# A step of an attention stage laid out anew: key, output and router projections in other slots, and the router's search with them

## The chip, the cores and the metric

The kernel runs on one core of a Trainium2 chip. The metric is the device time of one execution in microseconds (us), lower is better. Engines: TensorE (PE, matmul), VectorE (DVE), ScalarE (ACT), GpSimd (POOL), SyncE (SP, which here only issues DMAs).

## The reference, cut to what matters

One decoder layer over 16 batches of 256 tokens, width 256, three post-norm blocks in fp32:

```python
u = einsum('bld,nd->bln', x, B); h = scan(h = A*h + u)             # state
x = layernorm(x + h @ W.T + b)                                     # first norm: x1
q, k, v = proj(x, Wq, bq), proj(ctx, Wk, bk), proj(ctx, Wv, bv)    # 16 heads of 16
q, k = rotary(q), rotary(k)
scores = where(|i - j| <= 50, q @ k.T / 4, -1e9)
x = layernorm(x + softmax(scores) @ v @ Wo.T + bo)                 # second norm: x2
probs = softmax(silu(x @ router_w1) @ router_w2, over the tokens)
weights, tokens = top_k(probs, 64)                                 # for each of 16 experts
x = layernorm(x + scatter(weights * expert(x[tokens])))            # 16 gated MLPs
```

## The kernel before, in words

The kernel has two stages. `mixing` computes everything up to x2 and the router for the first eight batches; `experts` then runs 2 x 16 units of expert matmuls. The change lies in `mixing` alone.

`mixing` is a software pipeline written by hand. Its iteration is a **step** `i` (from -2 to 16), and each step has 16 **slots** `t`, one for a head. Every engine runs `step(it)` in a program of its own, strictly in order; semaphores join them. A name in `DELAY` says which batch an operation works on: U and Y (the state's input projection and its output projection) are two batches ahead of the heads, X (transpose of x1), K, Q, V one ahead, O (output projection), OX (transpose of x2) and R (router's first matmul) two behind. So K, Q, V exist in steps -1 to 14, U and Y in steps -2 to 13, and O, OX, R from step 2 on. Steps 2 to 9 are two passes of a hardware loop over four steps; the others are written out.

In slot `t` PE does, in this order: the scores of head t (`heads`, line 589, two matmuls into `score[t % 2]`, once DVE has finished head t-2); in slots 1, 5, 9, 13 the transpose of a group's maxima (`turn_maxima`, line 602); the transposed scores of head t-9 (`turned_heads`, lines 616 and 618); in slots 2, 6, 10, 14 a `gather` of probabilities times values (line 636); and then the slot's projection, if it has one.

All projections share two PSUM banks, `work[0]` and `work[1]`. `ORDER` (line 258) gives the cyclic order of the users of each bank, and `begin(it, name)` makes PE wait for `freed` of the user ahead of it in that order. These are freed by: K and Q by ACT's two bias activations (`biased`, line 841, `raw_k`, `raw_q`), X and OX by ACT's copies (line 856), O and Y by DVE's first addition in `statistics` (line 953), U by DVE's scan (line 1014), V by DVE's two additions into `vp` (line 1039), R by ACT's copy into `r1` (line 905).

The slots before: X 0, K 1, Q 3, O half in 4 and half in 7, U 5, Y 8, V 11, OX 13, R 15. The second norm's chain is: DVE `statistics` 8, ACT `estimate` 9 (log and exponential), POOL `inverse_deviation` (five operations on 128x2 elements), DVE `normalise` 11 (writes `x2cur`), PE OX 13, ACT x2T 14, PE R 15, ACT r1 15. `NORMAL` (line 318) holds these numbers, `DRAIN` those of the last step.

ACT's order in a slot: `keep_maxima` (slots 1, 5, 9, 13: copies the maxima that PE turned and issues a DMA with them), the exponential of head t-9 (line 787), and then the copies and bias activations of the slot: x1T in slot 1, K's bias in 2, Q's in 4, K's high half in 5, Q's in 7.

DVE's order: the maxima of head t (line 945, two pairs), in slots 3 and 11 the sums of the odd group (lines 994 to 1000), then the rotation of K (slot 3, lines 977 and 982) and of Q (5), the scan (6), the norms' statistics (O 8, Y 9) and normalisations (O 11, Y 13), and V (12).

POOL's order in a step: x1 plus a bias, x plus a bias, `cosine` and `rotate` of K, `cosine` and `rotate` of Q, `lower` of K, `lower` of Q (the low halves, line 468), the inverse sums of the even pair, the deviations of O and Y, the inverse sums of the odd pair. SP loads the next inputs, copies the halves of K and Q into their stacks (line 390) and stores x2 (line 423).

The router's search runs once inside this pipeline: ACT's silu over eight batches (step 10, slot 9), sixteen PE passes for the logits (step 11, slot 13, line 712), DVE's maximum (11, 14), ACT's exponential (12, 1), and eight rounds of `take_eight` on DVE (lines 121 to 124) from step 12 to 15.

Of the kernel before, what the change touches and what calls it, by code (L numbers as in the profile page):

```python
# [28 lines left out]
P = 128  # L29
NB = 16  # L30
S = 256
# [146 lines left out]
def mixing(nc, dram, keep):  # L178
# [5 lines left out]
    with ExitStack() as ctx:  # L184
# [73 lines left out]
        ORDER = (("X", "Q", "U", "Y", "OX"), ("K", "O", "V", "R"))  # L258
# [59 lines left out]
        NORMAL = {"O": (4, 7), "statistics": 8, "estimate": 9, "normalise": 11, "OX": 13, "x2T": 14, "R": 15, "r1": 15}  # L318
        DRAIN = {"O": (1, 2), "statistics": 2, "estimate": 3, "normalise": 5, "OX": 6, "x2T": 7, "R": 8, "r1": 9}

        def slot(it):
            return DRAIN if it.fixed and it.i >= NB else NORMAL

# [121 lines left out]
        def _(pool):  # L445
# [54 lines left out]
            def step(it):  # L500
                behind = it.batch(-1)
                if it.batch(0):
                    bias_residual(it)
                if there(it, "U"):

                    par = it.r % 2
                    pool.wait_ge(x_in[par], it.pairs(32, 2))
                    if not it.at_least(-1):
                        pool.wait_ge(const_in["b_mix"], 16)
                    else:  # L510
                        pool.wait_ge(x1_ready, it.lin(1, 2))
                    nc.gpsimd.tensor_tensor(xb[:], xin[par][:], b_mix[:].unsqueeze(1).to_broadcast([P, TT, D]),
                                            ALU.add).then_inc(xb_ready, 1)
                if it.fixed and it.i == -2:
                    pool.wait_ge(const_in["rope"], 32)
                    cosine(FIRST_KEYS, 0)
                    rotate(FIRST_KEYS, 0)
                if there(it, "K"):
                    if not hoisted(it):
                        cosine(it, 0)  # L520
                        rotate(it, 0)
                    cosine(it, 1)
                if there(it, "Q"):
                    rotate(it, 1)
                    if not hoisted(it):
                        lower(it, 0)
                    lower(it, 1)
                drain = it.fixed and it.i >= NB
                if drain and there(it, "O"):
                    inverse_deviation(it, "O")  # L530
                if behind:
                    inverse_sums(it, -2)
                if there(it, "O") and not drain:
                    inverse_deviation(it, "O")
                if there(it, "Y"):
# [30 lines left out]
        def _(pe):  # L566
# [99 lines left out]
            def step(it):  # L666
                for t in range(NH):
# [6 lines left out]
                    if t == 1 and there(it, "K") and not hoisted(it):  # L674
                        keys(it)
                    if t == 6 and it.fixed and it.i == -2:
                        keys(FIRST_KEYS)
                    if t == 0 and there(it, "X"):
                        first_use(it, "X", "ident")
                        pe.wait_ge(x1_ready, it.lin(1, 2))  # L680
                        transposed(it, "X", x1[(it.r + 1) % 4])
                    if t == 3 and there(it, "Q"):
                        first_use(it, "Q", "wq")
                        pe.wait_ge(freed["X"], uses(it, "X"))
                        project(it, "Q", wq, x1T)
                    if t in slot(it)["O"] and there(it, "O"):
                        n = slot(it)["O"].index(t)
                        if n == 0:
                            begin(it, "O")
                            pe.wait_ge(attnT_ready, it.lin(NPAIR, -NPAIR))  # L690
                        for g in range(NPAIR):
                            mm = nc.tensor.matmul(bank("O")[:, n * D:(n + 1) * D], attnT[it.r % 2][:, g, n * P:(n + 1) * P],
                                                  wo[:, g, :], start=(g == 0), stop=(g == NPAIR - 1))
                        if n == TT - 1:
                            mm.then_inc(ready["O"], 1)
# [11 lines left out]
                    if only(it, 11, t, 13):  # L707
                        pe.wait_ge(rw2_set, 1)
                        pe.wait_ge(silu_done, 1)
                        pe.wait_ge(freed["V"], uses(it, "V"))  # L710
                        for c in range(GB):
                            mm = nc.tensor.matmul(bank("R")[:, 0:S], rw2_placed[:, c, :], r1[:, c * S:(c + 1) * S],
                                                  start=(c == 0), stop=(c == GB - 1))
                        mm.then_inc(logits_ready, 1)
                    if only(it, NB - 1, t, 10):
# [16 lines left out]
                    if t == slot(it)["R"] and there(it, "R"):  # L732
                        if it.fixed and it.i == 11:
                            pe.wait_ge(logits_kept, 1)
# [7 lines left out]
                        mm.then_inc(ready["R"], 1)  # L742

# [16 lines left out]
        def _(act):  # L760
# [97 lines left out]
            def step(it):  # L858
                for t in range(NH):
# [3 lines left out]
                    if t == 2 and there(it, "K") and not hoisted(it):  # L863
                        biased(it, 0)
                    if it.fixed and it.i == -2 and t == 7:
                        biased(FIRST_KEYS, 0)
                    if t == 1 and there(it, "X"):
                        columns(it, "X", x1T)
                    if t in (7, 15):
                        keep_values(it, t)  # L870
# [6 lines left out]
                    if t == 5 and there(it, "K") and not hoisted(it):  # L877
                        heighten(it, 0)
# [6 lines left out]
                    if only(it, 10, t, 9):  # L885
# [4 lines left out]
                    if only(it, 12, t, 1):  # L890
# [25 lines left out]
        def _(dve):  # L916
# [68 lines left out]
            def step(it):  # L985
                for t in range(NH):
                    maxima(it, t)
                    if t in (3, 11) and has(it, group(t, 15)) and not only(it, NB, t, 11):

                        p = group(t, 15) // 2  # L990
# [10 lines left out]
                    if t == 3 and there(it, "K") and not hoisted(it):  # L1001
                        rotated(it, 0)
# [42 lines left out]
                    if only(it, 11, t, 14):  # L1045
# [4 lines left out]
                    if only(it, 12, t, 2):  # L1050
                        scale_probabilities(dve, route)
                    for n, (i, at) in enumerate(((12, 7), (12, 14), (13, 1), (13, 14), (14, 1), (14, 14), (15, 1), (15, 4))):
# [790 lines left out]
```

## Time and profile before

| | |
|---|---|
| median of 3 runs | 1072.51 us (1072.12 to 1072.58) |
| profiled execution: its own time, and its span | 1072.09 us, 1070.3 us |
| PE busy | 991.9 us (93%) |
| PE weight loads | 845.4 us (79%) |
| DVE busy | 729.6 us (68%) |
| POOL busy | 672.7 us (63%) |
| ACT busy | 591.3 us (55%) |
| mean granted PE clock | 0.975 |

The span is that of the profiled execution from its first to its last instruction; the own time is the device time of the same execution. Busy shares are means over both stages.

### The profile page before, as it was taken

What the parts mean: (1) busy time and instruction counts of PE and PEld (TensorE: products, weight loads), DVE (VectorE), ACT (ScalarE), POOL (GpSimd) and SP (SyncE); (2) the same over time, 40 slices, a digit from 0 to 9 for tenths busy, and PEclk for the clock granted to TensorE, in tenths of its full rate; (3) what the DMA queues carried; (4) which work ended last, traced back from release to release, by engine and by line L of the source; (5) the groups of instructions that cost most, each with busy time, mean ns of one, the idle gap of its engine ahead of it and who ended that gap; (6) DMA issues with size and microseconds to landing.
All of it is one profiled execution on the core that took longest, in us unless ns stands there. A gap on an engine that the chain in (4) does not pass through costs nothing.

```text
span 1070.3 us, 21269 instructions
## 1 busy us (share of the span) xinstructions
PE 991.9 (93%) x6436; PEld 845.4 (79%) x6436; DVE 729.6 (68%) x2168; ACT 591.3 (55%) x1234; POOL 672.7 (63%) x784
## 2 busy tenths in 40 slices
PE   4799999999989998879999999999999999999990
PEld 3578778777877877658898888888888888888880
DVE  4678888888877798757554787565556756765633
ACT  1155565556565555456656555555555556555642
POOL 5556666666666565267757665776666767666543
PEclk8899999999999999899999999999999999999995
DMA  6344344433333332525676666666676666666636
GB/s 191 84 103 98 100 106 103 103 99 102 102 101 97 85 81 70 182 94 168 156 223 124 160 141 168 136 158 152 160 218 158 141 155 149 147 155 143 184 54 176
DMA packets 114918, 142.56 MB, mean 133 GB/s; under 512 B 15104, under 2 KB 88064, under 8 KB 114688
## 3 DMA queue, kind: packets, MB, share of 16 engines
q1 hardware_dynamic: 86432, 105.56, 34.2%
q0 software_dynamic: 24576, 33.57, 18.1%
q10 hardware_dynamic: 3808, 2.22, 0.7%
q8 instruction: 45, 0.74, 0.3%
q14 instruction: 57, 0.47, 0.1%
HBM read 90.70 MB, written 29.36 MB: 112 GB/s over the span
## 4 chain that ended last, share of the span: by engine, by line
PE 52%; ACT 1%; DMA 1%; POOL 1%; issue 1%; DVE 0%; ACTq 0%; POOLq 0%; SPq 0%
PE gate_bank L1349 16%; PE attn L1349 16%; PE value_bank L1349 16%; PE turn_bank L1359 2%; DMA last<-acc_rows 0%; ACT last L1590 0%; DMA acc_rows<-y,slots_now 0%; PE attn L1432 0%; PE attn L1406 0%; POOL acc_rows L1294 0%; DVE stats L1627 0%; DVE hidden L1620 0%; ACTq L1594 0%; ACT w_hi L1482 0%; POOL rstd L167 0%
## 5 line engine op out<-in xcount | busy, mean ns | idle before, releaser
L1294 POOL DMA_INDIRECT acc_rows<-y,slots_now x128 | 205.6, 1607 | 137.4 <-issue 73.4
L787 ACT ACTIVATE probsT<-scoreT 128x356 f32<-128x356 f32 x256 | 117.7, 468 | 137.6 <-PE scoreT L618 113.3
L945 DVE CUSTOM_DVE_ANT_0 scored<-score,band 128x178 f32<-128x178 f32 x512 | 149.9, 337 | 63.3 <-PE score L589 59.4
L1620 DVE TENSOR_TENSOR hidden<-gate,value_bank 128x512 f32<-128x512 f32 x128 | 87.9, 687 | 152.7 <-ACT gate L1495 152.6
L1495 ACT ACTIVATE gate<-gate_bank 128x512 f32<-128x512 f32 x128 | 76.6, 598 | 188.3 <-PE value_bank L1349 188.3
L1349 PE MATMUL attn<-w_hi,h_hi 128*128 128x256 f32 x512 | 146.1, 285 | 0.2
L1349 PE MATMUL attn<-w_hi,h_lo 128*128 128x256 f32 x512 | 143.3, 280 | 0.0
L1349 PE MATMUL attn<-w_lo,h_hi 128*128 128x256 f32 x512 | 143.3, 280 | 0.0
L589 PE MATMUL score<-k_stack,q_stack 96*128 96x178 f32 x512 | 123.8, 325 | 7.2 <-DVE nmax L945 4.2
L589 PEld LDWEIGHTS score<-k_stack,q_stack 96*128 96x128 f32 x512 | 88.9, 194 | 37.1 <-DVE nmax L945 17.3
L618 PE MATMUL scoreT<-q_stack,k_stack 97*128 97x356 f32 x256 | 116.5, 456 | 0.0
L1612 DVE TENSOR_TENSOR h_lo<-hidden,h_hi 128x512 fp32r<-128x512 f32 x128 | 88.2, 689 | 21.5 <-ACT h_hi L1499 21.1
L1349 PEld LDWEIGHTS attn<-w_lo,h_hi 128*128 128x128 f32 x512 | 97.2, 190 | 3.2
L1349 PE MATMUL gate_bank<-k_stack,q_stack 128*128 128x512 f32 x384 | 99.1, 393 | 0.5 <-PEq L184 0.5
L1349 PEld LDWEIGHTS attn<-w_hi,h_hi 128*128 128x128 f32 x512 | 96.3, 188 | 3.8 <-ACT y L1509 0.3
L1349 PE MATMUL value_bank<-k_stack,q_stack 128*128 128x512 f32 x384 | 97.4, 389 | 0.0
L1349 PEld LDWEIGHTS attn<-w_hi,h_lo 128*128 128x128 f32 x512 | 96.2, 188 | 0.0
L1276 POOL DMA_INDIRECT rows<-x_rows,rows_now x64 | 76.7, 1199 | 28.0 <-issue 14.3
L1602 DVE TENSOR_TENSOR w_lo<-arena,w_hi 128x1024 fp32r<-128x1024 f32 x64 | 79.8, 1247 | 21.1 <-ACT w_hi L1482 20.9
L1499 ACT CAST h_hi<-hidden 128x512 fp32r<-128x512 f32 x128 | 78.9, 617 | 23.3 <-DVE hidden L1620 23.3
L616 PE MATMUL scoreT<-band_bf,ident_bf 128*128 128x356 bf16 x256 | 83.8, 327 | 5.9 <-ACT probsT L787 3.2
L1276 POOL DMA_INDIRECT arena<-x_rows,rows_now x60 | 71.6, 1193 | 26.9 <-issue 14.0
(214 smaller groups left out, 2374.9 us busy)
## 6 DMA issues: line engine op xcount, KB each, us to landing
arena<-in_w SPq DMA_DIRECT2D x96, 512.0 KB, 4.0
k_stack<-high_k SPq DMA_DIRECT2D x128, 64.0 KB, 2.2
q_stack<-high_q SPq DMA_DIRECT2D x128, 64.0 KB, 2.3
arena<-in_xT SPq DMA_DIRECT2D x16, 256.0 KB, 2.9
arena<-in_x SPq DMA_DIRECT2D x16, 256.0 KB, 3.1
arena<-in_cT SPq DMA_DIRECT2D x16, 256.0 KB, 3.7
k_stack<-low_k SPq DMA_DIRECT2D x64, 64.0 KB, 2.3
q_stack<-low_q SPq DMA_DIRECT2D x64, 64.0 KB, 2.2
```

The lines of the kernel that those rows point to most:

```text
L589: mm = nc.tensor.matmul(score[t % 2][:, q * SPAN:(q + 1) * SPAN], q_stack[par][0:TOP, t // 2, t % 2, q * P:(q + 1) * P], k_stack[par][0:TO ...
L616: nc.tensor.matmul(out, ident_bf[:], band_bf[:, k, :].unsqueeze(1).to_broadcast([P, 2, SPAN]), start=True, stop=False)
L618: nc.tensor.matmul(out, k_stack[par][0:TOP + 1, f, k * P:(k + 1) * P], q_stack[par][0:TOP + 1, f, :, k * FIRST:k * FIRST + SPAN], start=Fa ...
L787: nc.scalar.activation(probsT[g % 2][:, u % HG, :, :].rearrange("p a s -> p (a s)"), scoreT[u % 2][:, 0:2 * SPAN], ACT.Exp, scale=1.0 / DH ...
L945: op = nc.vector.tensor_tensor_reduce(scored[t % 2][:, q, :], score[t % 2][:, q * SPAN:(q + 1) * SPAN], band[:, q, :], -1.0, BIG, ALU.add, ...
L1276: nc.gpsimd.indirect_dma_start(rows[it.par][:, m, :], None, dram["x2"][it.h], bass.IndirectOffsetOnAxis(ap=now[:, m:m + 1], axis=0)).then_ ...
L1294: nc.gpsimd.indirect_dma_start(dram["acc"][c], bass.IndirectOffsetOnAxis(ap=now[:, m:m + 1], axis=0), y[m][:], None, compute_op=ALU.add).t ...
L1349: mm = nc.tensor.matmul(out, a[x], b[z], start=(n == 1), stop=(n == 3 * len(pairs)))
L1499: nc.scalar.copy(h_hi[it.par][:, f, :], hidden[f % 2][:]).then_inc(h_hi_ready, 1)
L1602: nc.vector.tensor_tensor(w_lo[it.par][n][:], raw[n], w_hi[it.par][n][:], ALU.subtract).then_inc(w_lo_ready[n], 1)
L1612: nc.vector.tensor_tensor(h_lo[it.par][:, f, :], hidden[f % 2][:], h_hi[it.par][:, f, :], ALU.subtract).then_inc(h_lo_ready, 1)
L1620: nc.vector.tensor_tensor(hidden[f % 2][:], gate[f % 2][:], value_bank[f % 2][:], ALU.mult).then_inc(hidden_ready, 1)
```

## The change: what it does

- K moves from PE's slot 1 to slot 0, behind X; ACT's bias of K from slot 2 to 1 (behind x1T), its high half from 5 to 3, DVE's rotation of K from slot 3 to 2.
- O moves whole into slot 2, with statistics in 3, estimate in 4, normalise in 7, OX in 9, x2T in 10, R in 13 and r1 in 14.
- OX moves from the first bank's order to the second's, behind O: K, O, OX, V, R.
- The odd group's sums move from DVE's slot 3 to 4.
- POOL does `lower` of K directly behind `rotate` of K, and the deviation of O ahead of `rotate` of Q.
- Router: silu from (step 10, slot 9) to (10, 2), logits from (11, 13) to (10, 15), with the bank wait on R instead of V and the wait on `logits_kept` now at K of step 11; maximum (10, 15), exponential (11, 4), scaling (11, 8), rounds at (11, 10), (12, 4), (12, 10), (13, 4), (13, 10), (14, 4), (14, 10), (15, 4); turn of the picks in step 15 from slot 10 to 11.

```diff
-        ORDER = (("X", "Q", "U", "Y", "OX"), ("K", "O", "V", "R"))
+        ORDER = (("X", "Q", "U", "Y"), ("K", "O", "OX", "V", "R"))
...
-        NORMAL = {"O": (4, 7), "statistics": 8, "estimate": 9, "normalise": 11, "OX": 13, "x2T": 14, "R": 15, "r1": 15}
+        NORMAL = {"O": (2, 2), "statistics": 3, "estimate": 4, "normalise": 7, "OX": 9, "x2T": 10, "R": 13, "r1": 14}
...
+        def odd_at(it):
+            return 3 if it.fixed and it.i >= NB else 4
...
 (POOL)
                     if not hoisted(it):
                         cosine(it, 0)
                         rotate(it, 0)
+                        lower(it, 0)
                     cosine(it, 1)
+                if there(it, "O"):
+                    inverse_deviation(it, "O")
                 if there(it, "Q"):
                     rotate(it, 1)
-                    if not hoisted(it):
-                        lower(it, 0)
                     lower(it, 1)
-                drain = it.fixed and it.i >= NB
-                if drain and there(it, "O"):
-                    inverse_deviation(it, "O")
                 if behind:
                     inverse_sums(it, -2)
-                if there(it, "O") and not drain:
-                    inverse_deviation(it, "O")
...
 (PE)
-                    if t == 1 and there(it, "K") and not hoisted(it):
-                        keys(it)
...
+                    if t == 0 and there(it, "K") and not hoisted(it):
+                        if it.fixed and it.i == 11:
+                            pe.wait_ge(logits_kept, 1)
+                        keys(it)
...
-                    if only(it, 11, t, 13):
-                        pe.wait_ge(rw2_set, 1)
-                        pe.wait_ge(silu_done, 1)
-                        pe.wait_ge(freed["V"], uses(it, "V"))
...
+                    if only(it, 10, t, 15):
+                        pe.wait_ge(rw2_set, 1)
+                        pe.wait_ge(silu_done, 1)
+                        pe.wait_ge(freed["R"], uses(it, "R") + FREED_EARLY["R"])
...
 (ACT)
-                    if t == 2 and there(it, "K") and not hoisted(it):
-                        biased(it, 0)
...
+                    if t == 1 and there(it, "K") and not hoisted(it):
+                        biased(it, 0)
...
-                    if t == 5 and there(it, "K") and not hoisted(it):
+                    if t == 3 and there(it, "K") and not hoisted(it):
                         heighten(it, 0)
...
-                    if only(it, 10, t, 9):
+                    if only(it, 10, t, 2):
                         act.wait_ge(freed["R"], GB + FREED_EARLY["R"])
...
 (DVE)
-                    if t in (3, 11) and has(it, group(t, 15)) and not only(it, NB, t, 11):
+                    if t in (odd_at(it), 11) and has(it, group(11 if t == 11 else 3, 15)) and not only(it, NB, t, 11):
...
-                    if t == 3 and there(it, "K") and not hoisted(it):
+                    if t == 2 and there(it, "K") and not hoisted(it):
                         rotated(it, 0)
...
-                    for n, (i, at) in enumerate(((12, 7), (12, 14), (13, 1), (13, 14), (14, 1), (14, 14), (15, 1), (15, 4))):
+                    for n, (i, at) in enumerate(((11, 10), (12, 4), (12, 10), (13, 4), (13, 10), (14, 4), (14, 10), (15, 4))):
```

## Rows read from the trace of the kernel before

**Rows 1.** The page's first line.

```profile
span 1070.3 us, 21269 instructions
```

**Rows 2.** PE's waits, 60 to 480 us: in total, times, longest.

```profile
PE work L657 <- DVE x2cur L969: 12.0, 13, 2.0
```

**Rows 3.** Engines' busy time (instructions) in two windows, granted clock, DMA share, GB/s.

```profile
243.30:269.40 26.10, 25.25 (x194) 20.91 (x193) 21.68 (x96) 15.47 (x42) 17.23 (x27) 1.00 0.39 102
447.30:453.20 5.90, 5.85 (x35) 4.66 (x36) 2.76 (x18) 2.78 (x7) 0.96 (x5) 0.50 0.12 51
```

**Rows 4.** PE's timeline in one step: start, length, instruction, count, idle before.

```profile
244.43 1.89 PE L649 MATMUL work<-arena,wk 128*128 128x256 f32 x8
...
258.67 0.55 PE L589 MATMUL score<-k_stack,q_stack 96*128 96x178 f32 x2
...
260.84 0.46 PE L589 MATMUL score<-k_stack,q_stack 96*128 96x178 f32 x2
...
265.35 0.66 PE L657 MATMUL work<-ident,x2cur 128*128 128x128 f32 x4 [0.85 <-DVE x2cur L969]
```

**Rows 5.** ACT's timeline in the same step.

```profile
245.80 0.58 ACT L856 COPY x1T<-work 128x512 f32<-128x512 f32 x1
...
247.24 0.83 ACT L841 ACTIVATE raw_k<-work,bk 128x256 f32<-128x256 f32 x2
...
259.36 0.26 ACT L798 CAST nmaxT<-attn 8x128 fp32r<-8x128 f32 x1 [1.36 <-PE attn L602]
...
260.46 0.47 ACT L787 ACTIVATE probsT<-scoreT 128x356 f32<-128x356 f32 x1 [0.84 <-PE scoreT L618]
```

**Rows 6.** PE's timeline in step 1, projection U.

```profile
70.40 1.96 PE L649 MATMUL work<-arena,wb 128*128 128x256 f32 x8 [0.76 <-ACT raw_q L841]
```

**Rows 7.** ACT's timeline in step 1.

```profile
69.42 0.83 ACT L841 ACTIVATE raw_q<-work,bq 128x256 f32<-128x256 f32 x2
```

**Rows 8.** DVE's timeline in the step of rows 4.

```profile
248.69 0.48 DVE L994 SCALAR_TENSOR_TENSOR mixed<-attn,halves,mixed 128x256 f32<-128x256 f32 x1
...
250.09 0.73 DVE L977 STREAM_SHUFFLE arena<-raw_k 128x512 f32<-128x512 f32 x1
250.85 0.69 DVE L982 TENSOR_TENSOR arena<-arena,sin 128x512 f32<-128x512 f32 x1
251.46 0.34 DVE L945 CUSTOM_DVE_ANT_0 scored<-score,band 128x178 f32<-128x178 f32 x1
...
252.52 0.73 DVE L977 STREAM_SHUFFLE arena<-raw_q 128x512 f32<-128x512 f32 x1
253.28 1.48 DVE L982 TENSOR_TENSOR arena<-arena,sin 128x512 f32<-128x512 f32 x1
...
255.21 1.25 DVE L1014 TENSOR_TENSOR_SCAN state<-acol,work 128x256 f32<-128x256 f32 x2
...
260.21 0.68 DVE L953 TENSOR_TENSOR pre_Y<-work,xb 128x512 f32<-128x512 f32 x1
...
262.13 0.34 DVE L945 CUSTOM_DVE_ANT_0 scored<-score,band 128x178 f32<-128x178 f32 x1
...
265.74 0.75 DVE L1039 TENSOR_TENSOR vp<-work,bv 128x256 f32<-128x256 f32 x2
```

**Rows 9.** PE's timeline: the turn of X in steps 10, 12 and 14.

```profile
295.50 0.60 PE L657 MATMUL work<-ident,x 128*128 128x128 f32 x4
...
353.91 0.60 PE L657 MATMUL work<-ident,x 128*128 128x128 f32 x4
...
407.56 0.60 PE L657 MATMUL work<-ident,x 128*128 128x128 f32 x4
```

**Rows 10.** PE's timeline in steps 10 and 11: behind the silu, and the logits.

```profile
318.36 0.33 PE L616 MATMUL scoreT<-band_bf,ident_bf 128*128 128x356 bf16 x1 [2.68 <-ACT probsT L787]
...
347.00 3.69 PE L712 MATMUL work<-r,rw_placed 128*128 128x256 f32 x16 [0.62 <-DVE vp L1039]
```

**Rows 11.** DVE's timeline in step 12: the first operation of a search round.

```profile
367.44 0.42 DVE L121 MAX8 top<-p_route 128x8 f32<-128x256 f32 x1
```

More of the change, by code:

```diff
@@ L685, in step @@
                         project(it, "Q", wq, x1T)
[L686 to L695, printed above, removed]
+                    for n in range(TT):
+                        if t == slot(it)["O"][n] and there(it, "O"):
+                            if n == 0:
+                                begin(it, "O")
+                                pe.wait_ge(attnT_ready, it.lin(NPAIR, -NPAIR))
+                            for g in range(NPAIR):
+                                mm = nc.tensor.matmul(bank("O")[:, n * D:(n + 1) * D], attnT[it.r % 2][:, g, n * P:(n + 1) * P],
+                                                      wo[:, g, :], start=(g == 0), stop=(g == NPAIR - 1))
+                            if n == TT - 1:
+                                mm.then_inc(ready["O"], 1)
                     if t == 5 and there(it, "U"):
@@ L706, in step @@
                         transposed(it, "OX", x2cur)
-                    if only(it, 11, t, 13):
-                        pe.wait_ge(rw2_set, 1)
-                        pe.wait_ge(silu_done, 1)
-                        pe.wait_ge(freed["V"], uses(it, "V"))
[L711 to L715, printed above, removed]
+                    if only(it, NB - 1, t, 11):
                         pe.wait_ge(route.picked, 1)
@@ L732, in step @@
                     if t == slot(it)["R"] and there(it, "R"):
-                        if it.fixed and it.i == 11:
-                            pe.wait_ge(logits_kept, 1)
                         if it.fixed and it.i == NB - 1:
@@ L742, in step @@
                         mm.then_inc(ready["R"], 1)
+                    if only(it, 10, t, 15):
+                        pe.wait_ge(rw2_set, 1)
+                        pe.wait_ge(silu_done, 1)
+                        pe.wait_ge(freed["R"], uses(it, "R") + FREED_EARLY["R"])
+                        for c in range(GB):
+                            mm = nc.tensor.matmul(bank("R")[:, 0:S], rw2_placed[:, c, :], r1[:, c * S:(c + 1) * S],
+                                                  start=(c == 0), stop=(c == GB - 1))
+                        mm.then_inc(logits_ready, 1)
             for i in (-2, -1):
@@ L889, in step @@
                         act.preload_act_table_set("natural_log_exp_and_others")
-                    if only(it, 12, t, 1):
+                    if only(it, 11, t, 4):
                         act.wait_ge(route.nmax_ready, 1)
@@ L987, in step @@
                     maxima(it, t)
-                    if t in (3, 11) and has(it, group(t, 15)) and not only(it, NB, t, 11):
-                        p = group(t, 15) // 2
+                    if t in (odd_at(it), 11) and has(it, group(11 if t == 11 else 3, 15)) and not only(it, NB, t, 11):
+                        p = group(11 if t == 11 else 3, 15) // 2
                         b = p % 2
@@ L1044, in step @@
                         normalise(it, "Y", x1[(it.r + 2) % 4], x1_ready)
-                    if only(it, 11, t, 14):
+                    if only(it, 10, t, 15):
                         dve.wait_ge(logits_ready, 1)
@@ L1049, in step @@
                         find_maximum(dve, route, route.p[:])
-                    if only(it, 12, t, 2):
+                    if only(it, 11, t, 8):
                         scale_probabilities(dve, route)
-                    for n, (i, at) in enumerate(((12, 7), (12, 14), (13, 1), (13, 14), (14, 1), (14, 14), (15, 1), (15, 4))):
+                    for n, (i, at) in enumerate(((11, 10), (12, 4), (12, 10), (13, 4), (13, 10), (14, 4), (14, 10), (15, 4))):
                         if only(it, i, t, at):
```

## The prediction

> **What bounds the kernel now.** I read the page first, then the waits of TensorE (PE) over the attention stage, then its busy time in one step, and last the timelines of that step engine by engine. Only the attention stage, the first 475 us or so of 1070.3, is touched [rows 1]. There PE's waits are few: the longest sum is the turn of the second norm (`OX`, line 657) waiting for VectorE (DVE) to write `x2cur`, 12.0 us in 13 times [rows 2]. One middle step lasts 26.10 us, of which PE is busy 25.25 at a granted clock of 1.00, that is 2.4 GHz [rows 3]; the missing 0.85 is that one wait, in slot 13 [rows 4]. So PE bounds a step, 0.85 us of it can be had, and any new wait in PE's own in-order program lengthens it in full. DVE is busy 21.7 us of the 26.1 and, read in its timeline, works without a gap from slot 3 to slot 15: it is the second bound, and little may be put in front of anything that PE waits for.
>
> **What the edits remove.** `OX` goes to slot 9, its normalise to slot 7. Its chain (statistics in slot 3, estimate in 4, POOL's five small operations, normalise in 7) starts six PE slots ahead of its reader, so I take the wait as gone: at most -0.85 a step. PE's own work is only reordered: 25.25 us stay.
>
> **Output projection behind the keys' bias: a new wait, +1.45.** `O` comes next to `K` in the chain of its bank, so `begin` makes it wait for `freed_K`, which ScalarE's (ACT) two bias activations give. Before, two slots and the query projection lay between; now PE does K as the last thing of slot 0 and wants the bank after slots 1 and 2. Those two (turned maxima, then a gather) are the same work as slots 9 and 10, which take 258.67 to 260.84 = 2.17 us after a projection [rows 4]. ACT cannot start on the bias by then: its program has `keep_maxima` of slot 1 first, which needs PE's transpose in slot 1, behind K. From that slot's start to the copy of the maxima is 259.36 - 258.67 = 0.69; from the copy to the exponential behind its DMA issue 260.46 - 259.36 = 1.10; the exponential is 0.47 long and the copy of x1T 0.58, each overlapped by about 0.1 by the next, so 0.37 and 0.48; the bias 0.83 [rows 5]; and from the start of such a bias to PE's next matmul 70.40 - 69.42 = 0.98, that is 0.15 of hand-over [rows 6, 7]. Sum 0.69 + 1.10 + 0.37 + 0.48 + 0.98 = 3.62, less 2.17: a wait of 1.45 us. Everything of the step is queued behind it on PE. Its lower bound, with a hand-over of nothing and an overlap of 0.1 more, is 1.2.
>
> **State projection behind the queries' bias: +0.76.** `U` in slot 5 waits for `freed_Q`, given by ACT in slot 4. Before, half of `O` filled slot 4. With the slot bare the trace has the case already: in step 1, which has no `O`, U starts at 70.40 after a wait of 0.76 for the bias of Q [rows 6]. I take 0.76; 0.65 to 0.80 are its ends.
>
> **Router's projection behind the values' copy: +0.84.** `R` moves from slot 15 to 13 and its bank is freed by DVE's copy of V in slot 12. DVE from slot 9: about 0.70 until a score is there, maxima 0.53 (half of 252.52 - 251.46), statistics of Y 1.92 (262.13 - 260.21), two maxima 1.06, the odd group's sums 1.40 (250.09 - 248.69), maxima 0.53, the copy of V 0.75 and 0.15 of hand-over: 7.04 [rows 8]. PE over the same slots: 265.35 - 258.67 - 0.85 = 5.83 up to the place where R now stands, plus 0.35 for the four transposes of `OX` that move into slot 9 (0.60 in their row, overlapped by the next) [rows 4, 9]: 6.18. The difference is 0.86, or 0.84 with roundings; lower bound 0.6.
>
> **What is hidden.** Keys' rotation in DVE's slot 2 waits for the same `freed_K` with maxima 3 behind it, whose scores PE has not made yet, since PE waits too: nothing. Its multiplication now falls together with POOL's cosine product of K. The pair for Q shows what that costs: 1.48 against 0.69 for K [rows 8]. The 0.79 ends before PE's late slot 3 has scores. The page "SBUF — State Buffer" of the Trainium skill, section "SBUF: two separate sides", calls the port that DVE and GpSimd share an exclusive lock, held for a whole instruction; by that rule the loser waits until the other ends, and this trace agrees (1.48 for an operation of 0.69 beside a POOL product). POOL: `lower` of K comes forward and waits for ACT's high half, with cosine of Q behind it, which has to wait for `freed_Q` anyway; the deviation of O before the rotation of Q holds that for some 1.5 us of small operations, and then the stacks of Q leave SP's queue about 2 us later, a step ahead of their use. SP has the same DMAs in the same order, the store of x2 last. All of that I cost at nothing; if the stacks came late, `heads` in slot 0 would wait.
> Y in slot 8 waits for DVE's scan. DVE from slot 3: 0.70 + 0.53 + 1.92 (statistics of O, now here) + 0.53 + 1.40 + 0.53 + Q's rotation (0.76 + 0.69, if POOL is not in the way) + 0.53 + 1.17 (the scan's 1.25 less an overlap) + 0.15 = 8.9 [rows 8]. PE: 25.25 less slot 0 (some 1.0 for a head and X, an estimate, and 1.54 for K, its 1.89 less the 0.35 that the next overlaps [rows 4]), less 2.17 and 1.54 for slots 1 and 2, less Y to the end of the step (1.54, the 6.18 above, and some 3.0 for R and slots 14 and 15, an estimate from slots 9 and 10 and four matmuls) leaves 8.3, with U's 0.76 some 9.1. So no wait, and no slack; with the rotation at 1.48 it is 0.6 to 0.75 a step.
>
> **Sum for a step:** 25.25 + 1.45 + 0.76 + 0.84 = 28.30 against 26.10: +2.2 us. Eight full steps (2 to 9): +17.6.
>
> **The router.** The turns of X stand at 295.50, 353.91 and 407.56 [rows 9]: steps 10 and 11 last 58.41 us, steps 12 and 13 53.65. Before, silu made PE wait 2.68 in step 10, and the sixteen logit matmuls took 3.69 us less some 0.3 of overlap [rows 10]. After: 2 x 28.30, logits 3.4, silu in slot 2 partly beside waits that are there anyhow, taken at 1.1 (0 and 2.68 as ends), one round: 62.35, so +3.9. A round of the search is three operations of about 0.42 = 1.25 us of DVE [rows 11]. In slot 10 it lies ahead of the copy of V, in slot 4 ahead of the scan, and neither chain has slack now: 1.25 each. Steps 12 and 13 have two each: 56.6 + 5.0 = 61.6, so +7.95. Before, the rounds were in slots 1, 7 and 14. Step 14 has no U and Y and was already held by DVE: about 0; step 15 and the drain: 0, within 2.6 either way; steps 0 and 1, where the keys' rotation one slot earlier eases DVE: about -1.
> 17.6 + 3.9 + 7.95 - 1 = 28.4, taken as 28. The profiled execution took 1072.09 us for a span of 1070.3; it becomes 1100.1. Its time is 0.4 under the median of 1072.51, so the median becomes about 1100.
>
> **Rivals.**
> *The three waits, and Y's too.* If POOL's small operations get in the way of Q's rotation, 0.7 us more in each of 12 steps: 1109.
> *Only O's wait counts.* If ACT and DVE are further ahead at Q and V than I reckon, a step costs 1.45 - 0.85 = 0.6: 12 x 0.6 + 5 for the router = 1085. Against it: step 1 shows U's wait.
> *PE's clock falls.* Half clock stood for 5.9 us in step 15, where PE had waited before [rows 3], and PE's work in such a stretch takes twice its time: about 3 us a step, 12 x 3 more = 1136. Against it: 0.85 in every step did not do it, nor 2.68 in step 10.
> *The other side.* ACT's second instruction behind the maxima's DMA issue could run while that is issued. It decides at the point where O's wait, U's and R's together are under 0.85 us a step: then 12.0 us come back, 1060. Against it: the exponential came 1.10 us behind the copy [rows 5].
>
> **How the numbers follow.** Main case 0.72, Y's wait too 0.08, only O's wait 0.08, the clock 0.04, the waits in balance 0.02 (1072), the faster side 0.06. The range 1084 to 1112 holds the first three, with the low ends of the waits (1.2 + 0.65 + 0.6 give +1.6 a step and 1091 in all); the main case alone is 1091 to 1107. A change within 0.2% (2.1 us) is about what a measurement of this kernel can't tell from none. Faster 0.06, same 0.02, slower 0.92.
>
> **What would show it.** Right: in the waits of PE, `work L692 <- ACT raw_k` about 1.4 us in 13 steps, `work L649 <- ACT raw_q` about 0.8 in 12, `work L740 <- DVE vp` about 0.8 in as many and 2 where there is a round in slot 10; x2cur's 12.0 nearly gone; a middle step of 28.3. Wrong: no wait ahead of L692, or a granted clock under 1.00 in the middle steps, or Y waiting for `state` in each step.

## The result, and the profile of the changed kernel

The changed kernel takes 1115.98 us (median of 4 runs, 1112.47 to 1121.17) against 1072.55 in the same session: a ratio of 1.0408 with a 95% interval of 1.0357 to 1.0458. It is slower, as forecast, but by 43 us and not by 28, and it lies outside the range of 1084 to 1112. Five rounds in another session gave 1115.61 (ratio 1.0401, 1.0383 to 1.0419). The profiled execution took 1112.87 us; its span answers to [rows 1]:

```profile
span 1111.1 us, 21271 instructions
```

PE's waits from 60 to 520 us (in total, times, longest), against [rows 2]:

```profile
PE work L694 <- ACT raw_k L841: 15.9, 13, 1.4
PE work L732 <- DVE vp L1039: 13.1, 13, 1.8
PE work L649 <- ACT raw_q L841: 11.4, 13, 1.9
PE score L589 <- DVE nmax L945: 8.1, 14, 1.5
```

L694 is now the output projection O and L732 the router's R. One wait of 12.0 us has gone but for 1.2, and three of 11 to 16 us have come, at the three places named in the forecast; waits for the maxima grew too, from 2.9 to 8.1 us, of which 4.5 lie in the last steps. In step 7, on PE's timeline (start, length, instruction, idle before and its releaser), they are 1.29, 0.76 and 0.76 us:

```profile
240.21 1.99 PE L694 MATMUL work<-wo,attnT 128*128 128x256 f32 x8 [1.29 <-ACT raw_k L841]
246.38 1.97 PE L649 MATMUL work<-arena,wb 128*128 128x256 f32 x8 [0.76 <-ACT raw_q L841]
259.54 1.10 PE L732 MATMUL work<-x2T,rw 128*128 128x256 f32 x4 [0.76 <-DVE vp L1039]
```

And the same step in a window (length, busy PE, PEld, DVE, ACT, POOL, granted clock, DMA share, GB/s), against [rows 3]:

```profile
234.70:263.00 28.30, 25.48 (x193) 20.98 (x192) 21.14 (x97) 15.27 (x42) 17.69 (x27) 1.00 0.37 93
```

28.30 us where 28.30 was forecast; the busy times of PE, DVE and POOL are within 0.6 us of what they were, and the clock is 1.00. ACT's order around K shows the chain of the first wait: the maxima's copy, the DMA issue, the exponential and the copy of x1T all stand ahead of K's bias, for which K had been ready since the end of slot 0.

```profile
237.37 0.26 ACT L798 CAST nmaxT<-attn 8x128 fp32r<-8x128 f32 x1 [1.45 <-PE attn L602]
237.66 0.65 ACTq L804 DMA_DIRECT2D q_stack<-nmaxT  x1
238.48 0.47 ACT L787 ACTIVATE probsT<-scoreT 128x356 f32<-128x356 f32 x1 [0.85 <-PE scoreT L618]
238.84 0.58 ACT L856 COPY x1T<-work 128x512 f32<-128x512 f32 x1
239.31 0.85 ACT L841 ACTIVATE raw_k<-work,bk 128x256 f32<-128x256 f32 x2
```

**Where the 40.8 us of span came from**, read from the turns of X (in slot 0 of each step, behind the scores of head 0) in both traces, with the forecast's term beside each:

| stretch | before | after | more | forecast |
|---|---|---|---|---|
| start to step 0 | 38.40 | 40.24 | +1.8 | 0 |
| step 0, step 1 | 23.41, 24.37 | 25.59, 26.33 | +4.1 | -1 |
| steps 2 to 9 | 209.32 | 227.55 | +18.2 | +17.6 |
| steps 10, 11 | 58.41 | 63.67 | +5.3 | +3.9 |
| steps 12, 13 | 53.65 | 62.16 | +8.5 | +7.95 |
| step 14 to the experts | 67.84 | 70.46 | +2.6 | 0 |
| experts | 594.9 | 595.1 | +0.2 | 0 |

So the largest term, steps 2 to 9, was right to 4%. Of the 12.4 us of span that the forecast lacks, 7 lie ahead of step 2, 2.6 in the last steps and 2 in steps 10 to 13. The rest of the miss, some 3 us, is that the profiled execution happens to be 3.1 us faster than its median. ACT in step 0 shows what steps 0 and 1 have in them:

```profile
47.07 0.62 ACT L851 CAST high_k<-raw_k 128x512 fp32r<-128x512 f32 x1 [3.57 <-POOL raw_k L466]
47.59 0.83 ACT L841 ACTIVATE raw_q<-work,bq 128x256 f32<-128x256 f32 x2
```

and PE in steps 0 and 1:

```profile
48.57 2.05 PE L649 MATMUL work<-arena,wb 128*128 128x256 f32 x4 [1.80 <-ACT raw_q L841]
...
76.77 1.10 PE L649 MATMUL work<-arena,wb 128*128 128x256 f32 x4 [1.86 <-ACT raw_q L841]
```

The high half of K, moved from ACT's slot 5 to slot 3, is a copy that waits for POOL to have rotated K. ACT stands 3.57 us in front of it, with Q's bias behind it, and U waits 1.80 and 1.86 us where it was 0.76 in step 1 before [rows 6]. In a middle step O hides this: its two us of work and its wait stand on PE ahead of Q, and ACT waits only 0.40 us for POOL.

```profile
243.64 0.62 ACT L851 CAST high_k<-raw_k 128x512 fp32r<-128x512 f32 x1 [0.40 <-POOL raw_k L466]
```

The 1.8 us ahead of step 0 are one projection of step -2, whose instructions the change doesn't touch. It took 1.99 us before and 3.78 after:

```profile
10.18 1.99 PE L649 MATMUL work<-arena,wk 128*128 128x256 f32 x8 [0.90 <-DMA wk<-in_WkT]
10.37 3.78 PE L649 MATMUL work<-arena,wk 128*128 128x256 f32 x8 [1.10 <-DMA wk<-in_WkT]
```

This is not the change's doing: below, runs of the changed kernel with the same program up to there have 1.99 (x4, whose step 0 starts at 38.27, as early as before) as well as 3.78 (x6). The granted clock is recorded as 1.00 there in both profiles, so they don't show why it took so long.

Step 11 has one more thing, which the forecast had only as a rival for every step: after R's wait of 1.79 us the granted clock went to half.

```profile
379.00:383.30 4.30, 4.30 (x31) 3.05 (x30) 1.76 (x10) 1.34 (x4) 4.14 (x5) 0.60 0.43 96
```

A mean of 0.60 is mostly the lower level, 1.2 GHz; 4.3 x 0.4 = 1.7 us of PE's work are lost. The repeated run has the same fall behind R's wait of step 11 (0.61 over 4.4 us), and between steps 2 and 13 none but this. The same wait of 1.79 stands in step 12 (at 411.00), and the clock there stays at 1.00.

### The profile page after: what moved, and what is told of

Read it like the earlier page. It is cut to its first block, busy times and chain, and to the rows that moved or that the text cites. A ratio compares the mean times of both kernels' runs of the same rounds, so it can differ in the third digit from the quotient of the medians.

```text
span 1111.1 us, 21271 instructions
## 1 busy us (share of the span) xinstructions
PE 1002.1 (90%) x6436; PEld 849.6 (76%) x6436; DVE 726.1 (65%) x2168; ACT 590.1 (53%) x1234; POOL 675.2 (61%) x784
## 4 chain that ended last, share of the span: by engine, by line
PE 49%; DMA 1%; POOL 1%; ACT 1%; issue 1%; DVE 0%; ACTq 0%; POOLq 0%; SPq 0%
PE attn L1349 16%; PE gate_bank L1349 15%; PE value_bank L1349 15%; PE turn_bank L1359 2%; DMA last<-acc_rows 0%; ACT last L1590 0%; DMA rows<-x_rows,rows_now 0%; DMA acc_rows<-y,slots_now 0%; PE attn L1432 0%; POOL rows L1276 0%; PE attn L1406 0%; POOL acc_rows L1294 0%; DVE stats L1627 0%; DVE hidden L1620 0%; ACTq L1594 0%
## 5 line engine op out<-in xcount | busy, mean ns | idle before, releaser
L589 PE MATMUL score<-k_stack,q_stack 96*128 96x178 f32 x512 | 121.5, 320 | 12.1 <-DVE nmax L945 9.4
L589 PEld LDWEIGHTS score<-k_stack,q_stack 96*128 96x128 f32 x512 | 91.6, 196 | 37.3 <-DVE nmax L945 20.7
```

The source lines that it names most:

```text
L589: mm = nc.tensor.matmul(score[t % 2][:, q * SPAN:(q + 1) * SPAN], q_stack[par][0:TOP, t // 2, t % 2, q * P:(q + 1) * P], k_stack[par][0:TO ...
```

## Experiments

The theory called 1 is that the new time is waits for what stands ahead of a releasing instruction in its engine's program: ACT's order for O and U, DVE's for R, the router's rounds in the late steps. The one called 3 is that K's high half in ACT's slot 3 makes steps 0 and 1 long. Each expectation states the rival. All medians and ratios are against the kernel before in the same session; "step" is a middle step's length from its profile.

| run | median, us | ratio | 95% interval | step, us |
|---|---|---|---|---|
| x0_changed_again | 1115.61 | 1.0401 | 1.0383 to 1.0419 | 28.33 |
| x1_key_bias_first | 1100.09 | 1.0252 | 1.0231 to 1.0274 | 26.94 |
| x2_query_bias_first | 1119.31 | 1.0434 | 1.0413 to 1.0455 | 28.34 |
| x3_router_slot_14 | 1119.88 | 1.0443 | 1.0412 to 1.0474 | 28.6 |
| x4_rounds_back | 1103.73 | 1.0305 | 1.0256 to 1.0354 | 28.32 |
| x6_both_biases_first | 1106.15 | 1.0316 | 1.0263 to 1.0370 | 27.05 |
| x7_high_half_slot_5 | 1130.47 | 1.0557 | 1.0511 to 1.0603 | 30.03 |
| x8_keys_alone | 1073.01 | 1.0014 | 0.9993 to 1.0036 | 26.25 |
| x9_norm_before_odd_sums | 1085.80 | 1.0120 | 1.0097 to 1.0143 | 26.92 |
| x10_keys_and_norm_ahead | 1088.64 | 1.0147 | 1.0122 to 1.0171 | 27.08 |
| x11_bias_and_rounds | 1086.63 | 1.0131 | 1.0103 to 1.0158 | 26.94 |
| x12_bias_rounds_high_early | 1084.87 | 1.0121 | 1.0094 to 1.0148 | 26.94 |

**The changed kernel again.** 

> The changed kernel unaltered, once more, to see how its time spreads. Theory 1 (three waits of PE plus those of the search rounds, at a full clock): about 1113 us in nearly all executions, step 5 to step 6 in 28.3 us, O's wait 13 x 1.25. Theory 2 (the rest of the loss is a granted clock that falls in some executions, since PE now waits more): again some executions near 1120, with a mean granted clock near 0.963 instead of 0.972, and the half-speed stretches lie in the start-up steps or in the steps with search rounds.

Measured: 1115.61, its profiled execution 1118.53 with a span of 1116.7. It is 5.6 us longer than the first profile, 4.2 of it ahead of the X of step 2 (96.38 against 92.16); a middle step is the same 28.33. In its step 1 the clock was 0.94, where it was 1.00 in the first, and in step -1 0.58 over 21.30 us, where it was 0.85 over 17.66. So both theories have a part: the three waits are in both profiles, and what scatters is the clock of the start, as the second had it. A total is only good to some 3 us.

**O's wait: K's bias ahead of the maxima.**

```diff
                 for t in range(NH):
+                    if t == 1 and there(it, "K") and not hoisted(it):
+                        biased(it, 0)
                     if t in (1, 5, 9, 13):
                         keep_maxima(it, t)
```

> The changed kernel, with ScalarE's bias of K ahead of the copy of the maxima in slot 1. Theory 1: O's wait was ScalarE's order (copy of the maxima, DMA issue, exponential, x1T, then the bias); with the bias first it ends 0.3 + 0.98 us after slot 1 starts, against 2.17 us until PE wants the bank: O's wait goes from 1.25 in 13 steps to nothing, a middle step from 28.3 to about 27.1 us, and the time falls by 14 to 17 us to about 1098. Rival (VectorE bounds the step by now): the wait at O goes, but waits for the maxima, for the scan or for V's copy grow by as much, and the time falls by under 5 us.

Measured: 15.5 us gained, the step 26.94. PE's waits from 95 to 355 us have no O any more:

```profile
PE work L649 <- ACT raw_q L841: 8.0, 10, 1.2
PE work L732 <- DVE vp L1039: 7.0, 9, 0.9
```

Theory 1 holds for O: the wait was the order of ACT's slot 1. And it bears on theory 3 by itself: K is rotated sooner, so in step 1 ACT waits 0.98 in front of the high half and not 2.65, U waits 0.8 and not 1.9, and the step takes 24.47 us and not 26.33. In step 0 it did not help: there ACT waits 3.32, and U 1.81 as before.

```profile
68.87 0.84 ACT L841 ACTIVATE raw_k<-work,bk 128x256 f32<-128x256 f32 x2 [1.51 <-PE work L649]
73.29 0.62 ACT L851 CAST high_k<-raw_k 128x512 fp32r<-128x512 f32 x1 [0.98 <-POOL raw_k L466]
```

The clock took part of the gain back in this profile: its mean is 0.95, 0.90 and 0.94 in steps 10, 12 and 13, where the changed kernel has 1.00, and steps 10 and 12 are 1.2 and 1.8 us longer than there; step 11, where the changed kernel's clock fell, has 1.00 and is 2.7 us shorter.

**U's wait: Q's bias ahead of the exponential.** The edit is the same for `t == 4` and `biased(it, 1)`, ahead of `exponentials(it, t)`.

> The changed kernel, with ScalarE's bias of Q ahead of the exponential in slot 4. Theory 1: U's wait (0.76 in 13 steps, 1.9 and 1.2 in some) goes, since the bias then ends 0.3 + 0.98 us after slot 4 starts and U is wanted after 1.5: a middle step goes from 28.3 to about 27.6, the time falls by 7 to 11 us. Rival (VectorE's scan holds Y): U starts earlier, but Y then waits for the scan by the same 0.7 us, and the time falls by under 3 us.

Measured: nothing gained, 3.7 us lost. U's wait of 0.76 is gone; 0.16 for maxima and 0.47 for Y have come, which the same step of the changed kernel doesn't have, and R's grew a little. PE's timeline in one middle step:

```profile
242.72 1.99 PE L694 MATMUL work<-wo,attnT 128*128 128x256 f32 x8 [1.30 <-ACT raw_k L841]
252.11 0.46 PE L589 MATMUL score<-k_stack,q_stack 96*128 96x178 f32 x2 [0.16 <-DVE nmax L945]
253.38 1.97 PE L649 MATMUL work<-ww,state 128*128 128x256 f32 x8 [0.47 <-DVE state L1014]
262.08 1.10 PE L732 MATMUL work<-x2T,rw 128*128 128x256 f32 x4 [0.80 <-DVE vp L1039]
```

Theory 1 falls for U, the rival holds: DVE is no further on when U starts sooner, so Y and the maxima wait for it. The forecast had said of Y "no wait, and no slack"; that is what is seen here. DVE even lost time: x2cur's normalisation, 0.73 us in the middle steps of the changed kernel, takes 1.68 to 2.24 here, beside POOL's low half of Q. The four steps where it takes 2.19 or more (2, 5, 6 and 9) are each some 0.6 us longer than in the changed kernel; that is 2.4 of the 3.7 us.

**R's wait: R in slot 14, r1 in 15** (two numbers in `NORMAL`).

> The changed kernel, with R in slot 14 and its copy in slot 15. Theory 1: R's wait for V's copy (0.78 in a middle step, 1.79 in those with a search round in slot 10) goes or shrinks to under 0.4, and the time falls by 8 to 13 us. Rival (VectorE runs late by then whatever PE waits for): the wait comes back as one for the maxima in slot 14 or 15, and the time stays within 3 us.

Measured: nothing gained, 4.3 us lost. The wait for `vp` is gone; R's bank is now freed late for the next user, K in slot 0, and O still waits:

```profile
239.90 1.97 PE L649 MATMUL work<-arena,wk 128*128 128x256 f32 x8 [0.67 <-ACT r L905]
245.04 1.99 PE L694 MATMUL work<-wo,attnT 128*128 128x256 f32 x8 [1.29 <-ACT raw_k L841]
```

So with K, O, OX, V and R on one bank, neither place tried is free for R: in slot 13 it comes too soon behind V, in 14 too close to K.

**The rounds back where they were.**

```diff
-  ((11, 10), (12, 4), (12, 10), (13, 4), (13, 10), (14, 4), (14, 10), (15, 4))
+  ((12, 7), (12, 14), (13, 1), (13, 14), (14, 1), (14, 14), (15, 1), (15, 4))
```

> The changed kernel with the rounds of the router in the slots that they had before (the last one in slot 4 of step 15, the others in slots 7, 14, 1, 14, 1, 14, 1). Theory 1 (the places of the rounds cost the late steps): R's wait of 1.79 us in the steps with a round in slot 10 falls back to 0.78, and Y's wait after the round in slot 4 goes; steps 12 and 13 fall from 31.08 us to about 29, and the kernel gains 4 to 6 us against the changed one's 1115.6. Rival (VectorE's work is the bound of those steps wherever a round stands): the same VectorE time is lost in other slots, steps 12 and 13 stay at 30.5 or more, and the time stays within 1.5 us of the changed kernel's.

Measured: the ratio falls from 1.0401 to 1.0305, about 10 us, twice what was expected. PE's waits on its timeline in step 12, of the changed kernel:

```profile
399.34 0.46 PE L589 MATMUL score<-k_stack,q_stack 96*128 96x178 f32 x2 [0.42 <-DVE nmax L945]
400.61 1.97 PE L649 MATMUL work<-ww,state 128*128 128x256 f32 x8 [0.47 <-DVE state L1014]
408.33 0.46 PE L589 MATMUL score<-k_stack,q_stack 96*128 96x178 f32 x2 [0.17 <-DVE nmax L945]
411.00 1.10 PE L732 MATMUL work<-x2T,rw 128*128 128x256 f32 x4 [1.79 <-DVE vp L1039]
```

And of this one, behind its U; Y and the maxima no longer make PE wait:

```profile
406.70 1.10 PE L732 MATMUL work<-x2T,rw 128*128 128x256 f32 x4 [1.23 <-DVE vp L1039]
```

Theory 1 holds for the rounds: steps 12 and 13 go from 31.08 each to 28.62 and 28.01. The rest was not in the expectation: step 11 goes from 31.17 to 28.51 (one round less, and no fall of the clock), and the stretch from step 14 to the experts from 70.46 to 68.10, which is nearly all of the 2.6 us that the forecast had put at nothing.

One more thing stands in this profile. The clock fell in step 6, behind waits that the changed kernel has there too, and O's projection took 3.68 us instead of 1.99; the step is 1.8 us longer than there.

```profile
210.83 3.68 PE L694 MATMUL work<-wo,attnT 128*128 128x256 f32 x8 [0.86 <-ACT raw_k L841]
```

**Both biases first, Q's rotation behind the scan.**

> The changed kernel with ScalarE's bias copy of the keys first in slot 1, that of the queries first in slot 4, and VectorE's rotation of the queries behind the scan in slot 6, so that it isn't in the way of the state. Theory 1: the waits of O (1.3) and of U (0.76) are both gone, a middle step takes 26.3 to 26.6 us, and the kernel about 1092. Rival (VectorE's order is what decides once O's wait is gone): U's 0.76 comes back as waits for vp, the state or the maxima, a middle step stays at 27.0 and the kernel at 1100 or above.

Measured: 1106.15, a step of 27.05. The rival's number, but not the wait it names. U and Y no longer wait; the second norm does, and R as before:

```profile
247.86 0.66 PE L657 MATMUL work<-ident,x2cur 128*128 128x128 f32 x4 [0.49 <-DVE x2cur L969]
254.55 1.10 PE L732 MATMUL work<-x2T,rw 128*128 128x256 f32 x4 [0.73 <-DVE vp L1039]
```

The 0.49 comes from DVE's normalisation, which takes 1.46 us where the changed kernel has 0.73; it now runs beside POOL's rotation of Q (246.06 on POOL).

```profile
246.35 1.46 DVE L969 TENSOR_SCALAR x2cur<-pre_O,mv_O,rstd_O 128x256 f32<-128x256 f32 x2
```

0.49 + 0.73 over the 25.25 of PE's work makes 26.5; the window has PE busy for 25.78 of 27.04, so half a microsecond is lost where the records show no wait, and its cause is open. U's 0.76 was given up for nothing in either form.

**K's high half back in slot 5.**

> The changed kernel with ScalarE's copy of the high half of the keys back in slot 5, where it was before. Theory 3 (in steps 0 and 1 ScalarE stands behind that copy for 3.6 and 2.7 us until GpSimd has rotated the keys, and the queries' bias copy comes late for it): U's wait in steps 0 and 1 falls from 1.8 us to 0.5 to 0.8, and the kernel gains 2 to 4 us against the changed one's 1115.6; a middle step stays at 28.3. Rival (steps 0 and 1 are longer for the clock alone): X of step 2 comes as late as in the changed kernel (92 to 96 us), and the time stays within 1 us.

Measured: 1130.47, the slowest of all. The first part of the expectation came true: U no longer waits in steps 0 and 1, and step 0 takes 23.34 us where it took 25.59, of which 1.6 are idle time; step 1 takes 25.85 for 26.33, since in it maxima (1.9 us) and Y (0.5) now wait for DVE. But each middle step is 1.7 us longer, which neither theory had: 1.1 in a new wait and 0.6 in PE's busy time (26.08 for 25.46). POOL's timeline there:

```profile
156.39 1.27 POOL L466 TENSOR_TENSOR raw_k<-rope_k,arena 128x512 f32<-128x512 f32 x1 [0.70 <-DVE arena L982]
162.82 1.52 POOL L471 TENSOR_TENSOR low_k<-raw_k,high_k 128x512 fp32r<-128x512 f32 x1 [5.16 <-ACT high_k L851]
164.30 1.28 POOL L459 TENSOR_TENSOR rope_q<-raw_q,cos 128x512 f32<-128x512 f32 x1
165.66 0.22 POOL L167 TENSOR_SCALAR rstd_O<-mv_O 128x2 f32<-128x2 f32 x1
...
166.78 0.19 POOL L175 TENSOR_TENSOR rstd_O<-guess_O,newton_O 128x2 f32<-128x2 f32 x1
```

What follows on DVE, whose normalisation waits for that last line:

```profile
167.09 1.58 DVE L969 TENSOR_SCALAR x2cur<-pre_O,mv_O,rstd_O 128x256 f32<-128x256 f32 x2 [1.69 <-POOL rstd_O L175]
```

And on PE, which waits for the normalisation:

```profile
168.72 0.66 PE L657 MATMUL work<-ident,x2cur 128*128 128x128 f32 x4 [1.10 <-DVE x2cur L969]
```

POOL's low half of K now stands ahead of the deviation of O and waits 5.16 us for ACT's high half. So the move from slot 5 to 3 costs in steps 0 and 1 and is what lets the norm's turn stand in slot 9 without a wait: a part of the change that pays for another part.

**The keys alone.** K in PE's slot 0, its bias in ACT's slot 1, its rotation in DVE's slot 2; everything else as before.

> The kernel before with one part of the change alone: K in slot 0 on TensorE, its bias copy in slot 1, its rotation in slot 2 on VectorE; the output projection stays in slots 4 and 7, its norm's turn in slot 13, the router as before. Theory 1 (the loss is that O stands whole in slot 2 behind K's bias copy): no wait of O, a middle step stays within 0.3 us of 26.1, and the kernel takes 1072 to 1077. Rival (the copies and rotations alone crowd ScalarE and VectorE): a middle step takes 26.7 or more, and the kernel 1082 or more.

Measured: 1073.01, no difference that can be told; the step is 26.25, with the wait for x2cur still there (11.9 us in 13 times). Theory 1 holds for the middle step: the move of the keys alone costs at most 0.15 us. The loss there lies in what was put behind them. That the totals agree so well is in part luck in this profile: steps 10 and 12 are 0.9 and 1.8 us longer than before, and the stretch from step 14 to the experts takes 63.05 us for 67.84, at a clock of 0.95 for 0.90.

**Could the old wait be had more cheaply?** The kernel before, with the normalisation of O ahead of the odd sums in DVE's slot 11.

> The kernel before with one line of VectorE's order changed: in slot 11 the normalisation into x2cur stands ahead of the two odd sums. Theory 5 (the wait of 0.85 us for x2cur that the kernel before has in a middle step is a matter of VectorE's order): the wait goes, the odd sums come 0.7 us later and nobody waits for them, a middle step takes 25.25 to 25.7 us, and the kernel 1060 to 1067. Rival (GpSimd's last Newton step ends at 263.3, so VectorE would now stand still for it, and VectorE is nearly the bound): the wait shrinks by half at most and comes back in front of the next maxima, a middle step stays at 25.9 to 26.1, and the kernel within 2 us of the one before.

Measured: 13 us slower, a step of 26.92. The wait for x2cur is gone, and this stands in one middle step:

```profile
270.15 0.46 PE L589 MATMUL score<-k_stack,q_stack 96*128 96x178 f32 x2 [1.16 <-DVE nmax L945]
...
272.83 1.13 PE L740 MATMUL work<-x2T,rw 128*128 128x256 f32 x4 [0.35 <-ACT x2T L856]
```

Both theories fall, the rival less far. DVE does the odd sums and the normalisation in one block, and the maxima of head 12 come behind it in either order. The scores of head 14, which PE does right after OX, wait for those maxima. In the kernel before PE waited 0.85 for x2cur and the maxima were nearly done by then (they start at 265.21 and 265.47, the scores at 265.88); take the first wait away and 1.16 for the second is seen. Steps 2 to 9 have 6.8 of the 14.0 us of span that this costs. Step 11 has 2.1 (the clock is 0.95 there for 1.00) and the stretch from step 14 to the experts 3.5 (0.87 for 0.90); what set these isn't shown.

> The kernel before with the keys in slot 0 (as in the run with the keys alone, 1073.0) and the normalisation into x2cur ahead of the odd sums. Theory 5: as in the run with the order alone, 7 to 10 us less than 1073, so 1063 to 1066. Rival (with the keys in slots 0 to 2 VectorE has no idle time left): no gain, 1071 or more.

The same on top of the keys alone: 1088.64 for 1073, the same wait of 1.16, a step of 27.08. So this order doesn't get the 0.85 us back there either.

**The two gains together.** Both diffs above (K's bias first, rounds back).

> The changed kernel with the two edits that gained by themselves: ScalarE's bias copy of the keys first in slot 1 (-15.5 us by itself) and the router's rounds where they were (-11.9 by itself). If the two losses are apart, their sum: 1115.6 - 27.4 = 1088, a middle step at 27.0, steps 12 and 13 at 27.3 or less. Rival (they share a cause, the crowding of VectorE): less than the sum, 1093 or more.

Measured: 1086.63, a step of 26.94, steps 12 and 13 at 27.4 and 26.8. The losses add, as theory 1 has it, and the rival falls. The sum even comes out 1.6 us better than 15.5 + 11.9; the clock is 1.00 in steps 2 to 13 here, which it was not in either run alone.

**And the high half late in steps 0 and 1 only** (`t == (5 if it.fixed and it.i in (0, 1) else 3)`).

> The same, with ScalarE's copy of the high half of the keys back in slot 5 in steps 0 and 1 alone. With that copy back in slot 5 in every step, steps 0 and 1 were 2.25 and 0.5 us shorter and each middle step 1.7 longer. Theory 3: 2 to 3 us less than the run before it in this call, about 1085 to 1086, X of step 2 at 88 to 90 us. Rival (the gain of step 0 was the clock's phase): within 1 us of it.

Measured: 1084.87, 1.8 us less, with intervals that overlap. Step 1 is 24.47 against 24.51; in step 0, which is 2.5 us shorter, U's wait of 0.50 goes, but the difference is all in PE's busy time (19.76 for 22.41 us, at a clock of 0.92 for 0.79). So this run doesn't tell what is left of theory 3's loss from scatter. In step 0 that differs between profiles of the same instructions: with K's bias first U waits 1.81 us in x1 and 0.50 in x11. No version beat the kernel before, whose 1072 us stays 13 us below the best version with O in slot 2. One step of x12 shows why: the two waits that are left cost more than the 0.85 that was removed.

```profile
260.07 1.97 PE L649 MATMUL work<-arena,wb 128*128 128x256 f32 x8 [0.76 <-ACT raw_q L841]
...
273.24 1.10 PE L732 MATMUL work<-x2T,rw 128*128 128x256 f32 x4 [0.77 <-DVE vp L1039]
```

## Why the prediction was right in kind and wrong in size

**The step: right.** The terms for O, U and R were 1.45, 0.76 and 0.84; they measured 1.29, 0.76 and 0.76, and -0.85 for x2cur came in full. A step took 28.30 to 28.33 for 28.30 forecast. That it agrees so closely is luck: the three waits came 0.24 short together, and PE's busy time, forecast as unchanged, 0.23 over (25.48 for 25.25). What was costed at nothing inside the step held: K's multiplication took 0.96 us, not the 1.48 taken from Q's, and Q's 0.69. The run with K's bias first shows that O's wait is caused as told. That U's and R's waits are "removable" by the same means was no part of the forecast, and the runs show that they aren't.

**Y without a wait and without slack: right.** In the middle steps it waits once, 0.18 us in step 6; with a round in slot 4 it waits 0.47, with U 0.76 sooner 0.47.

**"Steps 0 and 1: about -1": the step that failed.** The forecast looked there only at DVE's eased rotation, and costed ACT's high half by what waits for it on POOL, never by what stands behind it on ACT itself: Q's bias. Its own remark that POOL's `lower` "waits for ACT's high half" had the pair; the wait of the high half for POOL's rotation, on the engine that frees Q's bank, was the one to follow. In middle steps O covers it, so it was missed by reading a middle step and carrying it to the first two, which have no O. Measured: +4.1 us in steps 0 and 1 in the profiled execution. By U's waits 1.3 in step 0 (1.80 for 0.49) and 1.1 in step 1 (1.86 for 0.76) are this mechanism: with the high half late both are gone, and with the bias early that of step 1 is back at 0.75. The rest is PE's busy time (+0.9 and +0.4, in step 0 with a clock of 0.87) and 0.6 more of waits for maxima in step 1 (1.4 for 0.8).

**The start: mis-sized.** 1.8 us ahead of step 0 and some 3 us between profile and median were costed at nothing. The first is K's first projection at 3.78 us for 1.99, instructions that are the same in both kernels. Over the runs X of step 0 comes at 38.27 to 42.61, and where the changed kernel runs again it comes at 42.55, with a clock of 0.58 in step -1. So this is scatter of the start and not the change; why it scatters is open.

**The router: 11.85 forecast, 13.8 measured.** Steps 12 and 13 (1.25 us for each of four rounds) were right: taking the rounds out of slots 4 and 10 gave back 2.5 and 3.1 us. Steps 10 and 11 were 1.3 too low. By the forecast's terms step 10 would take 32.8 us and step 11 29.55; they took 32.50 and 31.17, so the excess is in step 11, and the 1.7 us of the clock's fall are enough to account for it.

**The tail at 0, within 2.6: mis-sized.** "Step 14 was already held by DVE" was taken as a reason for no cost. With the rounds back 2.36 of the 2.62 us came back, so their places did cost there. The repeated run of the changed kernel has 70.36, the two other runs with the rounds back 68.29 and 68.10. In the waits 0.9 is seen: PE waits 4.5 us for maxima there against 3.6 with the rounds back. The other 1.5 are in PE's busy time (57.24 for 55.78), at a mean clock of 0.88 for 0.90; that the rounds' places set the clock is not shown.

**Rivals.** Y's wait in every step, only O's wait, and the clock's fall in every step didn't happen. Between steps 2 and 13 the changed kernel's clock fell once; its variants show it elsewhere (x4 in step 6, x1 in 10, 12 and 13), so a part of each difference between single runs is the clock's, and no run isolates what sets it. The other side (ACT free to run beside the issue of its DMA) is refuted by the row of `nmaxT` above: the next exponential starts 1.11 us behind the copy, as in [rows 5], though the scores that it reads were done by 237.65.

## What to carry to other kernels

An instruction moved forward on its engine has to be followed in two directions: who waits for its result, and what stands behind it on its own engine while it waits for its input; and this in the first and last steps of a pipeline too, where the work and waits that cover it in the middle are missing. A wait on an in-order engine often hides a second one for the same busy engine: before you pay for its removal, ask what the next instruction would wait for, and try the removal by itself. When a new order costs time, swap single pairs in it: of 43 us lost here, 29 were two orders (one bias copy, eight rounds) that had nothing to do with the idea.

## What the runs showed that I had not expected

- The order inside a block of VectorE's work decided the wait: swapping two items inside it removed a wait of 0.85 us and made a step 0.8 us longer (1.16 and 0.35 came).
- The same wait of 1.79 us was followed by half clock in step 11 (0.60 over 4.3 us, and 0.61 in the repeated run) and by full clock in step 12.
- x2cur's normalisation, which the kernel before does in 0.73 us (at 264.57), took 1.58 us when it ran beside POOL's rotation of Q (167.09 on DVE, 166.93 on POOL, in the run with the high half in slot 5).
- The same eight matmuls at the start took 1.99 us in one profile and 3.78 in another, which moved all that follows by 1.8 us.
